# A graph-attention layer whose step order on TensorE is changed: row units set between masks and scores

## The reference

```python
qkv = layer_norm(x, g1, be1) @ w_qkv           # 4096 x 384
q, k, v = qkv split, each (4096, 8 heads, 16)
scores = jnp.einsum('nhd,mhd->hnm', q, k) * SCALE
scores = jnp.where((adj != 0)[None], scores, -jnp.inf)
attn = jax.nn.softmax(scores, axis=-1)
out = jnp.einsum('hnm,mhd->nhd', attn, v).reshape(n, DIM)
x = x + out @ w_proj + b_proj
h2 = layer_norm(x, g2, be2)
x + jax.nn.gelu(h2 @ w1 + b1) @ w2 + b2
```

## Time and profile before

| what | value |
|---|---|
| median of 3 runs | 1720.45 us (1720.43 to 1721.51) |
| the profiled execution, its own time | 1722.52 us |
| its span in the trace | 1720.7 us |
| mean granted TensorE clock | 0.982 of full speed |
| PE busy | 1593.7 us, 93% |
| DVE busy | 1419.5 us, 82% |
| ACT busy | 1297.3 us, 75% |
| POOL busy | 1169.9 us, 68% |

### The profile page before, as it was taken

One profiled execution on the slowest core, in us unless ns is written; L12 is line 12 of the kernel. 1 busy time (PEld: TensorE's weight loads), 2 busy tenths in 40 slices (PEclk: granted clock), 3 DMA queues, 4 the chain that ended last, 5 costly groups with the idle time before them and its releaser, 6 DMA issues. The chain is left out here.

```text
span 1720.7 us, 46494 instructions
## 1 busy us (share of the span) xinstructions
PE 1593.7 (93%) x17016; PEld 492.6 (29%) x17016; DVE 1419.5 (82%) x4490; ACT 1297.3 (75%) x1425; POOL 1169.9 (68%) x1092
## 2 busy tenths in 40 slices
PE   6989999999999999999999999999999999999986
PEld 3422222323223232323323232232323232232313
DVE  6888989887998889887899879997898879998701
ACT  4547878788787878778787878778787877878783
POOL 4945487569856798558865789567874698567541
PEclk9879999999999999999999999999999999999998
DMA  7710046202460045400452035500462024500000
GB/s 211 184 50 2 2 134 123 69 2 61 130 129 15 2 117 131 84 2 26 147 109 53 2 97 130 106 2 12 136 127 59 2 63 140 105 2 2 8 1 13
DMA packets 174176, 119.85 MB, mean 70 GB/s; under 512 B 140238, under 2 KB 154447, under 8 KB 173948
## 3 DMA queue, kind: packets, MB, share of 16 engines
q1 hardware_dynamic: 163196, 108.49, 26.1%
q10 hardware_dynamic: 10752, 8.39, 1.7%
HBM read 77.25 MB, written 6.04 MB: 48 GB/s over the span
## 5 line engine op out<-in xcount | busy, mean ns | idle before, releaser
L817 DVE CUSTOM_DVE_ANT_0 masked_out<-ring_ps,row_mask 128x512 bf16<-128x512 f32 x2048 | 1312.6, 688 | 143.5 <-PE ring_ps L1039 102.4
L782 ACT ACTIVATE probs<-score_ps,score_scale 128x1024 f32<-128x1024 f32 x1024 | 1089.0, 1112 | 334.7 <-PE score_ps L1210 326.7
L564 POOL TENSOR_TENSOR probs<-probs,keep 128x1024 int32<-128x1024 int32 x256 | 605.0, 2364 | 281.4 <-ACT probs L782 269.9
L1103 PE MATMUL pv_ps<-probs,v_ones 128*17 128x512 f32 x4096 | 543.6, 598 | 4.4 <-POOL probs L564 3.3
L1039 PE MATMUL ring_ps<-k_stack,q_stack 51*64 51x512 f16 x4096 | 485.7, 397 | 15.1 <-DVE row_max L817 14.4
L1210 PE MATMUL score_ps<-q_stack,k_stack 51*64 51x512 f16 x4096 | 374.0, 391 | 19.7 <-ACT probs L782 0.3
L1195 PE MATMUL score_ps<-mask_t,ident_bf 64*64 64x512 bf16 x3072 | 281.3, 388 | 49.6 <-ACT probs L782 31.6
L1039 PEld LDWEIGHTS ring_ps<-k_stack,q_stack 51*64 51x64 f16 x4096 | 164.9, 104 | 493.1 <-DVE row_max L817 443.4
L1210 PEld LDWEIGHTS score_ps<-q_stack,k_stack 51*64 51x64 f16 x4096 | 117.3, 104 | 217.6 <-PE score_ps L1195 185.9
L817 DVE DVE_READ_ACCUMULATOR2_ANT row_max<- 128x1 f32 x2048 | 170.4, 83 | 0.0
L1195 PEld LDWEIGHTS score_ps<-mask_t,ident_bf 64*64 64x64 bf16 x3072 | 91.5, 105 | 211.2 <-ACT probs L782 163.0
(11 more groups left out here) (121 smaller groups left out, 811.7 us busy)
## 6 DMA issues: line engine op xcount, KB each, us to landing
adj_in<-adj SPq DMA_DIRECT2D x128, 512.0 KB, 4.2
q_stack<-q_dram SPq DMA_DIRECT2D x42, 64.0 KB
mask_t<-row_mask SPq DMA_TRANSPOSE x128, 3.4
xq<-xnT_dram ACTq DMA_DIRECT2D x8, 256.0 KB, 2.6
x_res<-x ACTq DMA_DIRECT2D x8, 256.0 KB, 4.5
out<-rows ACTq DMA_DIRECT2D x8, 256.0 KB, 2.5
xnT_dram<-attn ACTq DMA_DIRECT2D x4, 256.0 KB, 3.7
xnT_dram<-halves ACTq DMA_DIRECT2D x4, 256.0 KB, 2.1
```

The costliest lines, as they stand in the source:

```text
L564: nc.gpsimd.tensor_tensor(view, view, keep[:, KEPT.index(m), :].unsqueeze(1).broadcast_to([128, 2, TILE]), ALU.mult).then_inc(probs_masked, 1)
L782: nc.scalar.activation(probs[:, (2 * g + n) % SLOTS, :], score_ps[:, half:half + 2, :].rearrange("p a n -> p (a n)"), ACT.Exp, scale=score ...
L817: nc.vector.tensor_tensor_reduce(out=masked_out[:, place % 3, :], in0=ring_ps[:, place % 3, :], in1=row_mask[:, j, ch * 512:(ch + 1) * 512 ...
L1103: last = nc.tensor.matmul(pv_ps[32 * k:32 * k + HD + 1, :], v_ones[:, block_of(g, b), 2 * p + a, :], probs[:, (2 * g + b) % SLOTS, a * TIL ...
```

## The change

On PE the order within a step becomes: masks 0 (even steps only); row 0, row 1; scores 0; masks 1; row 2; scores 1; row 3; values. So in an even step the first masks stand ahead of the first two row units, and in every step one row unit stands between the second masks and their scores. All other engines' queues are as they were.

As scores 0 of a pair's first step no longer stand behind the wait of masks 1, an explicit wait on `score_taken` is added there: the two rows of `q_stack` that ACT copies for this pair of heads must have been written.

```diff
@@ in scores(g, n) @@
                     else:
                         pe.wait_ge(masks_set, i * MASKED + masked_before(g, n) + 1)
+                    if g % QUARTER == 0 and n == 0 and not (p == 0 and isinstance(i, int) and i == 0):
+
+                        at = max(ACT_PLACE[SHIFT_STEP[p, jj]] for jj in range(2)) - SCORE_PLACES * (p == 0)
+                        pe.wait_ge(score_taken, SCORES.before(i) + SCORES.upto(bcd, at))
                     first = K_FIRST + 128 * (m % 4)
@@ in body(i, par, b, c, d) @@
                 for g in range(STEPS):
-                    for x in range(UNITS // 2):
-                        row(g, x)
-                    if c and pool_step(g):
+
+
+                    if c and not pool_step(g):
+                        masks(g, 0)
+                    row(g, 0)
+                    row(g, 1)
+                    if c:
                         scores(g, 0)
                         masks(g, 1)
+                    row(g, 2)
+                    if c:
                         scores(g, 1)
-                    elif c:
-                        masks(g, 0)
-                        masks(g, 1)
-                        scores(g, 0)
-                        scores(g, 1)
-                    for x in range(UNITS // 2, UNITS):
-                        row(g, x)
+                    row(g, 3)
                     if g in act_fills and g % 2 == 1:
                         act_fill(i, bcd, g, act_fills[g])
```

## The result

The changed kernel takes 1734.73 us (median, 1734.61 to 1735.80) against 1720.95 for the kernel before on the same chip: slower by 13.8 us, ratio 1.008 (95% interval 1.0067 to 1.0094). The forecast was 1744, slower, with a range of 1722 to 1764: the direction and the mechanism held, the size was 23.6 us forecast and 13.8 measured.

The account below looks back on a forecast made before the run. Bound: a PE-DVE loop of 2.66 us per even step. Per tile +7.7 - 2.6 - 2.0 + 0.5 = +3.6, over 7.67 tiles +27.6, less 4 at the end: +23.6 on 1722.5, forecast 1744 us, range 1722 to 1764.

Parts of the forecast that it names:

- The loop as the bound: Even step: row 0 to DVE, row 3's weights, values, next row 0; 0.59 + 0.75 + 0.33 + 0.99 = 2.66 us.
- Row 2 between masks 1 and scores 1 gains nothing by itself: Odd steps: row 2 fills 0.24 of PE idle, but the step falls only to 2.66; gain 2.0 us a tile.
- Masks 0 on the loop: Even steps: masks 0 ahead of row 0 add their 0.24 issue to each of 32 steps, 7.7 us a tile.
- What absorbs it: Even steps held by something other than the loop give back part of the masks' cost; together 2.6 us a tile.
- Steps 4, 20 and 52: Even steps after ACT's copies of `pv_ps`: scores 0 no longer wait behind masks 1; 2.90 instead of 3.09 each.
- Step 30: Even step whose values wait for POOL; the 0.24 of masks 0 vanish there.
- The fills: Twelve ACT fills (4 up, 8 shift) start some 0.04 later against the odd step's row 0; 0.5 us a tile lost.
- held by a full ACT: At ACT's fills: the third exponential, so held before, is now held by the odd step's scores 0; some 0.04 later.
- The steps without row units: Last 21 steps of the last tile: scores 0 no longer behind masks 1; 0.4 per pair, ten pairs, 4 us gained.
- The added wait: Before a pair's first scores, on an ACT copy: costed at nothing; if binding, up to 1 us a tile, 8 in all.
- A: Rival: PE's issue sets the tile's pace, so its gaps count and masks 0 cost nothing; faster, 1700 us; chance 0.13.
- C: Rival: single row units cost more; row 3 ready at 1.44, not 1.34, each step 0.10 longer; 1793 us; chance 0.10.

Follow-up runs that it names:

- experiment 3: Kernel before with one move alone: masks 0 of even steps ahead of row 0, no row unit between masks and scores; 1742.18 us.
- experiments 5 and 6: Changed kernel and kernel before, each with the DVE maxima taken over only 256 of 512 columns; 1669.50 us and 1688.18 us.
- experiment 1: Changed kernel with odd steps put back to the order of before, even steps in the changed order; 1736.68 us.
- experiment 2: Changed kernel with even steps put back to the order of before, odd steps in the changed order; 1718.41 us.
- experiment 8: Changed kernel with the values' matmuls cut into two halves of 256 queries, nothing issued between them; 1736.38 us.
- experiment 7: Changed kernel with the values cut into two halves of 256 queries and, in some 45 of 64 steps, the next step's row 0 between them; 1833.28 us.

## Why the prediction was right, and where its sizes were off

*The loop as the bound* was right. Its four terms came back as 0.57, 0.75, 0.34 and 0.98; experiment 3 shows that the one move onto it makes the whole loss, experiments 5 and 6 that a shorter DVE instruction opens it.

*Row 2 between masks 1 and scores 1 gains nothing by itself*: right in that the loop sets 2.66. But I credited the odd steps' 2.0 us under this heading, and experiments 1 and 2 give it to ACT's earlier start. The size was 1.8.

*Masks 0 on the loop*: forecast 32 x 0.24 = 7.7 us a tile, measured 0.22 to 0.23 in the steps that the loop holds, 7.2 for 32. Behind the masks DVE starts 0.57 after row 0's issue, not 0.59.

*What absorbs it*: forecast 2.6, measured 7.2 - 4.2 = 3.0. Steps 4, 20 and 52 changed by -0.20, -0.20 and -0.21, as worked out. Step 30 fell from 3.25 to 2.89: the wait for POOL did not just hide the masks, it went.

*The fills*: forecast +0.5, measured 0. Up steps last 3.95 before and after, shift steps without a second fill 2.98. The step that failed is "held by a full ACT": the third exponential starts 0.75 after the odd step's row 0 in both traces (777.05 after 776.30, 780.06 after 779.32), so the odd step's scores 0 held it in the kernel before too.

These terms make +2.4 instead of +3.6 a tile, the largest part of the miss: over seven tiles 16.5 instead of 25.2. With tile 8 and the end (-0.2) and the start (-4.1) that is, but for rounding, the 12.3 of the spans.

*The steps without row units*: forecast -4, against +2.4 for the 43 steps ahead of them; together -0.2 instead of -1.6. ACT's trains:

```profile
1680.30 4.29 ACT L782 ACTIVATE probs<-score_ps,score_scale 128x1024 f32<-128x1024 f32 x4 [0.69 <-PE score_ps L1214]
1685.28 1.11 ACT L782 ACTIVATE probs<-score_ps,score_scale 128x1024 f32<-128x1024 f32 x1 [0.69 <-PE score_ps L1214]
```

4.98 apart instead of 5.08: the chain that I had put near 4.9 binds at once. Most pairs gain only 0.1; step 43 gains 0.5, steps 46 and 47 together 0.5, steps 52 and 53 0.6. The stretch from step 43 to step 63 shrinks by 1.9 (53.2 to 51.4), against +2.3 over the 43 steps ahead of it. The last 0.6 lie behind step 63, in a stretch that lasts 32.7 to 34.6 in the traces of the step orders; I count them as no gain of the order.

*The start* was a term I had left out. From the first transposes of the shift to step 4 the kernel before takes 26.1 us and the changed one 23.7: 2.4 gained (experiment 8, which has the changed order, takes 23.7 again). Experiment 1, with the even steps' order alone, takes 24.4, and experiment 2, with the odd steps' alone, 25.2, so both halves of the change pay there. TensorE's granted clock there is 0.50 of full speed (1.2 GHz) in both traces; PE has masks and scores to issue beside the rows, and no values.

```profile
115.00:120.00 5.00, 4.94 (x34) 1.49 (x32) 5.00 (x17) 1.17 (x2) 0.00 (x0) 0.50 0.01 3
120.00:125.00 5.00, 5.00 (x44) 1.45 (x42) 4.61 (x16) 4.04 (x4) 2.35 (x1) 0.50 0.00 0
```

(From 5 us windows of the changed kernel: span, busy PE, PEld, DVE, ACT and POOL, then the clock, the DMA share and GB/s.) In the kernel before, which is 1.7 us behind at this place, PE was busy for 4.40 of the 5.00 us from 120 to 125; the changed kernel is busy for 4.94 from 118.3 to 123.3. That the order pays here because values are absent is argued, not shown: no run changed the first steps alone.

*The added wait* costs nothing: even steps 0, 16, 32 and 48, which carry it, grew by 0.22, 0.23, 0.22 and 0.22 like the others.

Of the rivals, A (PE's issue sets the pace) is refuted by experiments 1 to 3. C did not come about: row 3 was ready by PE's order at 1.19 after row 0, where C had 1.44, and 0.13 before the bank was free. What row 2 alone costs is not to be read from its 0.24 (862.75 to 862.99): scores 1 follow masks 1 after 0.47 with the unit between them (862.52 to 862.99) and without it (experiment 1), so they wait for their masks. Where no masks are waited for, as in experiment 7, half of the scores starts 0.01 after a lone unit (904.44 and 904.45).

## What to carry to other kernels

Where two engines wait for each other through a small ring of buffers, walk once round the loop and add up the distances from start to start; as long as that walk takes longer than the engines' own order of issue, only work on it costs time. Work moved onto it cost 0.22 of its 0.24 us here, although the same engine had time to spare elsewhere in the step. A gap on the busiest engine is worth filling only if it lies on such a walk, and an order that feeds one engine earlier (ACT here) pays once the loop through the other is shorter. Before interleaving on TensorE, read what a change of matmul shape costs in the trace: here a second visit to the value products ate all that it saved, or more.

## What the runs showed of the hardware

- Row units and masks or scores (64-row, 64-column tiles) start 0.24 apart in groups of four. In front of the value products (128 rows, 17 columns) it is 0.32 to 0.33, for a group of four (861.38 to 861.70 in the earlier trace rows) and for a single row unit of two (863.37 to 863.70).
- Scores start 0.46 to 0.48 after the masks that they wait for, with a row unit between them or not. A row unit of two matmuls and two of the four score matmuls behind it can start together (904.44 and 904.45 in experiment 7).
- The value products of 512 queries take 0.98; cut into two halves back to back still 0.98 (899.87 to 900.85 in experiment 8); a half with a row unit behind it 0.56, a quarter 0.34.
- Waits of the weight loader overstate what a wait costs: for the masks they grew by 62 us although the gap had been filled.
